# Queue orders rewritten: the opening of a conditioned attention and convolution block on one core

## The reference

```python
# 1. conditional 1x1 mixing: a small MLP of cond gives 8 weights per batch
att = softmax(gelu(gelu(cond @ W0 + b0) @ W1 + b1) @ W2 + b2)
agg = einsum('bk,koi->boi', att, weight);  y = einsum('boi,bih->boh', agg, x) + att @ bias_k
# 2. attention within each row: 32 heads of width 32, one shared key and value
q, k, v = y @ Wq + bq, y @ Wk + bk, y @ Wv + bv
o = einsum('bsde,bse->bsd', softmax(q_d * k_e / sqrt(32)), v)
x = x + broadcast(o)                 # q is summed over its 32 heads
# 3. grouped convolution (9 taps, 4 groups) + context of cond + bias, then a 4-bit linear layer
u = conv(x, weight2) + cond @ c_weight + bias
x = x + u @ (scale * (unpack(packed) - zero_point)).T + ffn_bias
```

## Time and profile before

| | before |
|---|---|
| median of three runs | 423.92 us |
| lowest, highest | 418.14, 425.28 us |
| span of the profiled execution, first to last instruction | 422.5 us |
| PE busy in it | 408.1 us, 97% |
| DVE, POOL, ACT busy | 356.2, 357.4, 222.6 us |

### The profile page before, as it was taken

One profiled execution on the slowest core, in us unless ns is written; L12 is line 12 of the kernel. 1 busy time (PEld: TensorE's weight loads), 2 busy tenths in 40 slices (PEclk: granted clock), 3 DMA queues, 4 the chain that ended last, 5 costly groups with the idle time before them and its releaser, 6 DMA issues.

```text
span 422.5 us, 6627 instructions
## 1 busy us (share of the span) xinstructions
PE 408.1 (97%) x2135; PEld 346.0 (82%) x2135; DVE 356.2 (84%) x594; ACT 222.6 (53%) x472; POOL 357.4 (85%) x358
## 2 busy tenths in 40 slices
PE   5979999999899999999999999999999999999997
PEld 4869988888788888888888888888888888888886
DVE  2679899999989999998979999989889899983422
ACT  4522896644637653774273565645463556572700
POOL 6034998999899999999998999999998889999920
PEclk9998999999999999999999999999999999999999
DMA  8984869067956036663069472919083452716112
GB/s 315 406 341 141 325 219 322 3 205 278 311 197 242 5 111 223 166 212 95 36 201 369 135 302 78 346 23 310 5 305 122 110 221 57 273 44 234 52 51 101
DMA packets 24954, 79.13 MB, mean 187 GB/s; under 512 B 6088, under 2 KB 6728, under 8 KB 22984
## 3 DMA queue, kind: packets, MB, share of 16 engines
q1 hardware_dynamic: 24760, 78.32, 52.9%
q10 hardware_dynamic: 144, 0.13, 0.1%
HBM read 61.14 MB, written 17.30 MB: 186 GB/s over the span
## 4 chain that ended last, share of the span: by engine, by line
PE 72%; DMA 2%; POOL 1%; DVE 1%; issue 1%; SPq 0%; DVEq 0%; POOLq 0%
PE p_f L1520 48%; PE p_conv L1514 18%; PE p_sm L1479 5%; DMA o_c<-o_dram 1%; PE p_sm L1499 1%; DMA o_dram<-o_sb 1%; PE p_conv L1520 0%; POOL c_lo L555 0%; DVE prob L1061 0%; POOL xc L545 0%; POOL xn L564 0%; DVE rden L1110 0%; POOL xc L548 0%; POOL xc L546 0%; DVE xn L1140 0%
## 5 line engine op out<-in xcount | busy, mean ns | idle before, releaser
L1520 PE MATMUL p_f<-w_ffn,u_hi 128*128 128x512 f32 (+1 forms) x512 | 194.7, 391 | 0.0
L1520 PE MATMUL p_f<-w_ffn,u_lo 128*128 128x512 f32 (+1 forms) x512 | 194.5, 389 | 0.0
L781 ACT ACTIVATE u_sb<-p_conv,u_bias,cols_sb 128x128 f32<-128x128 f32 x256 | 94.9, 461 | 37.9 <-PE p_conv L1514 37.5
L1520 PEld LDWEIGHTS p_f<-w_ffn,u_hi 128*128 128x128 f32 x512 | 96.2, 188 | 20.7 <-DVE u_lo L1130 0.3
L1520 PEld LDWEIGHTS p_f<-w_ffn,u_lo 128*128 128x128 f32 x512 | 96.1, 188 | 20.1
L555 POOL TENSOR_TENSOR c_lo<-xc,c_hi 128x516 fp32r<-128x516 f32 (+1 forms) x68 | 83.9, 1244 | 5.2 <-POOL xc L548 1.9
L771 ACT ACTIVATE c_hi<-xc 128x516 fp32r<-128x516 f32 (+1 forms) x68 | 41.4, 611 | 69.7 <-POOL xc L548 69.7
L564 POOL TENSOR_TENSOR xn<-xn,bias_n 128x1024 f32<-128x1024 f32 x32 | 76.4, 2404 | 0.2
L545 POOL TENSOR_TENSOR xc<-xc,o_c 128x384 f32<-128x384 f32 (+1 forms) x68 | 58.0, 853 | 7.9 <-DMA o_c<-o_dram 5.2
L1140 DVE TENSOR_TENSOR xn<-p_f,xn 128x512 f32<-128x512 f32 x64 | 43.2, 675 | 21.9 <-PE p_f L1520 21.5
L571 POOL TENSOR_TENSOR xn<-xn,o_sb 128x1024 f32<-128x1024 f32 x32 | 60.9, 1920 | 0.3
(11 more groups left out here) (127 smaller groups left out, 480.2 us busy)
## 6 DMA issues: line engine op xcount, KB each, us to landing
xn<-xn_in_in SPq DMA_DIRECT2D x16, 1024.0 KB, 6.9
out<-xn SPq DMA_DIRECT2D x31, 512.0 KB, 5.6
xc<-xc_in_in SPq DMA_DIRECT2D x15, 1032.0 KB, 8.7
xt<-xt_in_in SPq DMA_DIRECT2D x11, 1024.0 KB, 7.6
o_c<-o_dram SPq DMA_DIRECT2D x15, 256.0 KB
xn<-xt_in_in SPq DMA_DIRECT2D x3, 1024.0 KB, 15.2
xn<-wq_in SPq DMA_DIRECT2D x5, 512.0 KB, 8.4
xt<-xt_in_in SPq DMA_DIRECT2D x4, 512.0 KB, 9.7
```

The costliest lines, as they stand in the source:

```text
L781: ins = eng.activation(u_sb[:, g % 2, i * P:(i + 1) * P], p_conv[g % 2][:, i * P:(i + 1) * P], ACT.Identity, bias=u_bias[:, g, bat:bat + 1 ...
L1520: return mm(ffn_ps(k, part), u[:, (k // TU) % 2, r, t * P:(t + 1) * P], w_ffn[:, r, at:end], **flags)
```

## The change

The same sums are computed, with the same tiles. What differs:

- **PE.** `keep_busy` writes to bank `p_conv[1]`. Six dummy products behind `turn_att` become fifteen single ones: one behind `mlp(0)`, seven behind `mlp(2)`, two behind `turn_att`, and two, two and one between the z products of tile 0. `context` goes to bank `p_ut[0]`, waits for the copies of the mixing matrices out of it, and moves behind the first half of unit 3. `z_first` and `z_second` no longer wait for `u_bias`. `mix_first` moves ahead of `z_second`, `read_flag` behind the first half of unit 4.
- **DVE.** `logits` stands ahead of `sum_heads(0)`, the flag behind the last head sum. The maxima of tile 0 stay in PSUM (`top()`) instead of going to the SBUF tile `top_own`. `low_nibbles` stands ahead of `score(1, 0)`.
- **ACT.** `copy_vk` between the second `gelu` and `exp_att`; all four `mix_rows` ahead of `z_copy_first`; `bias_of_u` behind `exp(0, 1)`; `exp(1, 0)` and the first conversion ahead of `z_copy(3)`.
- **POOL.** `ones` is set first. All four `add_o(0, g)` run ahead of `c_low(0, 0)`, and three `add_o(1, g)` ahead of `c_low(0, 2)`.
- **SP.** The convolution weights are loaded two places sooner, the second half of unit 0's convolution input ahead of `spread_first(0)`, `bias` later.
- **All queues** are written out to the end, without the loops, and differ from before in many places: the number of each kind of call is the same, save the dummies; x of units 11 to 13 and 15 is projected somewhat sooner among the linear tiles, and POOL's last three additions of o stand together at its end.

The diff, cut to what the text speaks of:

```diff
             load_tile(1, 0)
+            load_conv_weights()
             load_tile(1, 1)
             load_x(2)
-            load_conv_weights()
             load_x(3)
             load_x(4)
             load_packed()
             save_o(0, 0)
             load_c_first(0)
+            load_c_first(1)
             spread_first(0)
             load_x(5)
-            load_bias()
             load_x(6)
             save_o(0, 1)
-            load_c_first(1)
+            load_bias()
             spread_first(1)
+            load_n(0)
             load_x(7)
-            load_n(0)
             save_o(1, 0)
             load_c(1)
             save_o(1, 1)
             spread_o(1)
             load_x(8)
+            load_x(9)
+            load_x(10)
             load_c(2)
             load_n(1)
+            store(0)
...
+            eng.memset(ones[:, :], 1.0).then_inc(s_ones, 1)
             eng.memset(ident[:, :], 0.0).then_inc(s_ident, 1)
             eng.wait_ge(s_ident, 1)
             eng.affine_select(out=ident[:, :], in_=ident[:, :], compare_op=ALU.not_equal, fill=1.0,
                               base=0, pattern=[[-1, P]], channel_multiplier=1).then_inc(s_ident, 1)
-            eng.memset(ones[:, :], 1.0).then_inc(s_ones, 1)
...
             add_o(0, 2)
+            add_o(0, 3)
             c_low(0, 0)
             c_low(0, 1)
             subtract(1, 1)
-            add_o(0, 3)
-            c_low(0, 2)
-            c_low(0, 3)
             add_o(1, 0)
             add_o(1, 1)
             add_o(1, 2)
+            c_low(0, 2)
+            c_low(0, 3)
+            add_o(1, 3)
             c_low(1, 0)
             c_low(1, 1)
-            add_o(1, 3)
             c_low(1, 2)
             x_bias(0)
+            x_o(0)
             c_low(1, 3)
-            x_o(0)
             add_o(2, 0)
...
+            x_bias(30)
+            c_low(16, 2)
+            c_low(16, 3)
+            x_bias(31)
+            x_o(29)
+            x_o(30)
+            x_o(31)
...
-                    eng.activation(u_bias[:, g, :], p_conv[1][:, B * g:B * g + B], ACT.Identity, bias=cbs[:, g:g + 1], scale=sc).then_inc(s_ub, 1)
+                    eng.activation(u_bias[:, g, :], p_ut[0][:, B * g:B * g + B], ACT.Identity, bias=cbs[:, g:g + 1], scale=sc).then_inc(s_ub, 1)
 
             gelu(0)
             gelu(1)
+            copy_vk()
             exp_att()
             slices()
-            bias_of_u()
             keep_bias()
-            copy_vk()
             keep_mix_bias()
             mix_rows(0)
             mix_rows(1)
             mix_rows(2)
+            mix_rows(3)
             z_copy_first()
-            mix_rows(3)
             z_copy(0)
             exp(0, 0)
             exp_first()
             z_copy(1)
             z_copy(2)
             exp(0, 1)
+            bias_of_u()
+            exp(1, 0)
+            convert_weights(0, 0)
             z_copy(3)
-            convert_weights(0, 0)
             z_copy(4)
             c_high(0, 0)
-            exp(1, 0)
             c_high(0, 1)
             convert_weights(0, 1)
+            u_copy(0, 0)
+            u_copy(0, 1)
+            exp(1, 1)
             c_high(0, 2)
-            u_copy(0, 0)
-            z_copy(5)
-            u_copy(0, 1)
             c_high(0, 3)
-            exp(1, 1)
-            u_high(0, 0)
             convert_weights(1, 0)
             c_high(1, 0)
+            c_high(1, 1)
+            c_high(1, 2)
+            z_copy(5)
+            z_copy(6)
+            u_high(0, 0)
+            u_high(0, 1)
...
-                eng.tensor_tensor(top_of(0)[:, 0, :], top()[:, 0, :], top2[:, 0, :], ALU.max).then_inc(s_top_first, 1)
+                eng.tensor_tensor(top()[:, 0, :], top()[:, 0, :], top2[:, 0, :], ALU.max).then_inc(s_top_first, 1)
...
-                eng.tensor_tensor(prob[:, t, d, :], prob[:, t, d, :], down(top_of(a)[:, t, d]), ALU.subtract).then_inc(s_sub, 1)
+                eng.tensor_tensor(prob[:, t, d, :], prob[:, t, d, :], down((top() if a == t == 0 else top_of(a))[:, t, d]), ALU.subtract).then_inc(s_sub, 1)
...
-                eng.tensor_tensor(prob[:, 0, FIRST, :], prob[:, 0, FIRST, :], down(top_of(0)[:, 0, FIRST]), ALU.subtract).then_inc(s_sub_first, 1)
+                eng.tensor_tensor(prob[:, 0, FIRST, :], prob[:, 0, FIRST, :], down(top()[:, 0, FIRST]), ALU.subtract).then_inc(s_sub_first, 1)
...
+            logits()
             sum_heads(0)
-            logits()
             normal()
             sum_heads(1)
-            mark_inexact()
             sum_heads(2)
             sum_heads(3)
             sum_heads(4)
@@ -1174,6 +1400,7 @@
             sum_heads(6)
             sum_heads(7)
             sum_heads(8)
+            mark_inexact()
             bias_of_qkv(0)
             softmax_top_first()
             score_first()
@@ -1190,100 +1417,99 @@
             divide(0, 0)
             score(0, 1)
             softmax_top(1)
+            low_nibbles()
             score(1, 0)
-            low_nibbles()
             sum_exp(0, 1)
             times_v(0, 1)
             sum_v(0, 1)
             divide(0, 1)
+            sum_exp(1, 0)
             score(1, 1)
-            sum_exp(1, 0)
+            times_v(1, 0)
+            high_nibbles()
+            sum_v(1, 0)
+            divide(1, 0)
             softmax_top(2)
-            high_nibbles()
-            times_v(1, 0)
-            sum_v(1, 0)
+            sum_exp(1, 1)
             turn_u(0, 0)
-            divide(1, 0)
-            sum_exp(1, 1)
+            times_v(1, 1)
             turn_u(0, 1)
-            times_v(1, 1)
+            sum_v(1, 1)
             u_low(0, 0)
-            sum_v(1, 1)
-            turn_u(0, 2)
             u_low(0, 1)
             divide(1, 1)
+            turn_u(0, 2)
...
-                    mm(p_conv[0][:, 0:P], ones[:, :], ones[:, :], start=True, stop=True)
+                    mm(p_conv[1][:, 2 * P:3 * P], ones[:, :], ones[:, :], start=True, stop=True)
...
-                    eng.wait_ge(s_ub, G)
...
-                eng.wait_ge(s_ub, G)
...
                 eng.wait_ge(s_ctx, 1)
+                eng.wait_ge(s_mixt, 2)
                 for g in range(G):
-                    last = mm(p_conv[1][:, B * g:B * g + B], ctx_sb[:, g, :, :].rearrange("p r c -> p (r c)"), cond_sb, start=True, stop=True)
+                    last = mm(p_ut[0][:, B * g:B * g + B], ctx_sb[:, g, :, :].rearrange("p r c -> p (r c)"), cond_sb, start=True, stop=True)
                 last.then_inc(s_cb, 1)
...
             mlp(0)
+            keep_busy(1)
             mlp(1)
             mlp(2)
-            context()
+            keep_busy(1)
+            keep_busy(1)
+            keep_busy(1)
+            keep_busy(1)
+            keep_busy(1)
+            keep_busy(1)
+            keep_busy(1)
             turn_att()
-            keep_busy(6)
+            keep_busy(1)
+            keep_busy(1)
             mixing(0)
             mixing(1)
             mixing(2)
             mixing_bias()
             mixing(3)
-            read_flag()
             z_first(0)
             z_first(1)
             z_first(2)
             z_first(3)
+            keep_busy(1)
+            keep_busy(1)
             z_first(4)
             z_first(5)
+            keep_busy(1)
+            keep_busy(1)
             z_first(6)
+            keep_busy(1)
             z_first(7)
             col_sum(7)
+            mix_first()
             z_second()
-            mix_first()
             mix(0)
             project(1, 0)
             project(1, 1)
@@ -1665,97 +2050,98 @@
             project(2, 0)
             project(2, 1)
             project(3, 0)
+            context()
             project(3, 1)
             mix(2)
             project(4, 0)
+            read_flag()
             project(4, 1)
             project(5, 0)
             conv(0, 0)
+            conv(0, 1)
             project(5, 1)
-            conv(0, 1)
             project(6, 0)
+            project(6, 1)
             conv(0, 2)
-            project(6, 1)
             conv(0, 3)
             project(7, 0)
             conv(1, 0)
+            conv(1, 1)
             mix(3)
-            conv(1, 1)
-            conv(1, 2)
             linear(0, 0)
             linear(0, 1)
             linear(0, 2)
-            conv(1, 3)
...
```

More of the change, by code:

```diff
@@ L1796, in _ @@
             linear(9, 6)
+            mix(8)
+            conv(7, 0)
             linear(9, 7)
-            conv(7, 0)
-            conv(7, 1)
             linear(10, 0)
@@ new lines, in _ @@
+            linear(15, 1)
+            mix(11)
+            linear(15, 2)
+            linear(15, 3)
+            linear(15, 4)
+            linear(15, 5)
+            linear(15, 6)
+            linear(15, 7)
+            linear(16, 0)
+            linear(16, 1)
+            linear(16, 2)
+            linear(16, 3)
+            linear(16, 4)
+            linear(16, 5)
+            conv(10, 0)
+            linear(16, 6)
+            linear(16, 7)
+            linear(17, 0)
+            conv(10, 1)
@@ new lines, in _ @@
```

(19 more changed lines are left out.)

1118 lines of the change are left out of this document (803 added, 315 removed).

## The result

| | median, us | runs |
|---|---|---|
| kernel before, beside it | 421.03 | 4 (416.49 to 425.28) |
| changed kernel | 424.06 | 4 (422.35 to 424.25) |

The ratio is 1.0144, 95% interval 1.0106 to 1.0182: slower by 1.4%, less than the 2% named above, but with the whole interval above 1. The forecast was 418.0, with a range from 412.5 to 424. The profiled execution took 424.25 with a span of 422.5, which is also the span that the prediction was worked out from.

The account below looks back on a forecast made before the run. PE, busy 408.1 of 422.5 us, was taken as the bound, POOL and DVE close behind. Span: 422.5 - 4.9 (opening) - 0.9 (47 to 120) = 416.7; against the median 423.92 - 5.8 = 418.1, stated 418.0, range 412.5 to 424.

Parts of the forecast that it names:

- the 2% named above: Whole kernel: what a measurement can tell, here 8.5 us.
- The opening, step by step: Start to conv(1, 0): hand-worked new times, first mix 20.3 against 24.20, conv(1, 0) 53.7 against 58.65; PE 4.9 us ahead.
- that choice between two bounds: Opening, z products of tile 0: clock rises before the last sums, giving 19.2 to 20, not about 23 at low clock.
- the 0.9 of that term: From 47 to 120 us: half of 1.7 us of c_low waits taken away; bounds 0 and 1.7.
- From 120 on ... I take 0: Behind 120 us: PE has no idle time to lose; DVE's and POOL's idle time covers the new order, 0 us.
- the mark itself: Behind 120 us: PE idle time there was listed among the signs that the forecast is wrong.
- the offset to the median: Whole kernel: runs' median 1.4 us above the profiled span, lowest run 4.4 below; forecast taken against the median 423.92.
- The PSUM maxima: DVE's first subtraction in the opening: one operand in PSUM avoids POOL's split, 0.68 instead of 2.81, giving back 2.13 us.
- the second rival: Opening gains, middle takes it back: clock rises no earlier, POOL bounds 47 to 120; 421 to 423 us, chance 0.20.
- The slower rival: POOL's queue: c_low(0,2) late behind adds and a DMA trip, PE waits at conv(0,2); e.g. 433 us, chance 0.08.
- three engines are within 3% of one another: Whole kernel: argument against the rival that all of the gain arrives, 414.8 us by the median, chance 0.30.

Follow-up runs that it names:

- the second profile: Changed kernel run once more without an edit: median 423.44 us, the profiled execution 422.62 with a span of 420.8.
- The new opening by itself: Changed kernel's opening on every queue to about the first linear slots of tile 0, then the order of before: 418.14 us, ratio 0.9986 to before.
- The kernel with two fillers: Changed kernel with two of its fifteen dummy products, both behind turn_att: 425.62 us, ratio 1.0147 to before.
- for the sums: Changed kernel with add_o(u, 2) behind c_low(u, 0) and add_o(u, 3) behind c_low(u, 1) in every unit: 436.57 us, ratio 1.0416 to before.
- The order up to tile 13: Changed kernel's lists to linear(13, 7), about 215 us, then what remains in the order of before: 420.03 us, ratio 1.0030 to before.
- both edits: Kernel before plus five dummy products, context product behind project(3, 0) in another bank, bias_of_u behind exp(0, 1): 417.36, again 416.95 us.
- loosened waits alone: Kernel before with the context product behind project(3, 0) in another bank and bias_of_u behind exp(0, 1), no added dummies: 419.03 us, ratio 1.0010.
- u_high moved: Changed kernel with u_high(11, 2), (11, 3), (12, 3) and (13, 3) ahead of the next unit's c_high on ScalarE: 427.84 us, ratio 1.0244 to before.
- GpSimd's old list: Changed kernel with only GpSimd's list behind linear(13, 7) in the order of before: 435.09 us, ratio 1.0354 to before.
- SyncE's old list: Changed kernel with only SyncE's DMA queue behind linear(13, 7) in the order of before: 445.42 us, ratio 1.0613 to before.

## Why the prediction was wrong

**The opening, step by step: right.** The sums ended at 18.53 (predicted 18.6), the first mix came at 19.47 (20.3), the first subtraction took 0.68 (0.68), mix 1 came at 26.51 with 0.42 of idle time (26.9, 0.4), the first half of unit 5 at 39.77 with 0.51 (40.3, 1.3), conv(0, 0) at 42.69 with 0.92 (42.8, 0.7), conv(0, 2) with 0.30 (0.5 to 0.8), conv(1, 0) at 53.20 (53.7). The clock rose at 12.5, ahead of the last sums; that choice between two bounds was right. From conv(1, 0) to 120 us the waits for c_lo shrank from 1.7 to 0.7 (one, at 66 us), so the 0.9 of that term arrived as well.

**First failed step: "From 120 on ... I take 0".** Its reasoning was that the idle time of DVE and POOL, 18.4 and 12.3 us, would cover any new order. Idle time summed over 260 us covers nothing: what counts is whether each single hand-over is in time, and the new order has four that are not, behind 120 us. The term measures 4.17 us of stands and 1.7 of the clock's fall behind the last. With the lead of 5.45, the 0.9 and these two the sum is 422.5 - 5.45 - 0.9 + 4.17 + 1.7 = 422.0, against 422.5 measured; 0.5 is left over. The stands come back in the second profile (3.94 us), the fall doesn't, and nine of ten executions had none, so it is the stands that carry the loss. The prediction said that the new order could only add idle time here, and gave no upper bound for it. The diff reordered five lists behind 120 us, and each crossing in them could have been followed as those of the opening were. The prediction named the mark itself: idle time of PE after 120.

**Second failed step: the offset to the median.** The opening's gain was measured from one execution of before, whose clock rose at 22. The prediction saw that the rise was late, and that the lowest run lay 4.4 under this span, but took the lateness for a property of the code. It was a property of the execution: with the rise at 13, the same code has its first mix at 20.64 and conv(1, 0) at 52.45. Of the 4.73 by which the first mix came earlier, 3.56 comes with the early rise in the old order too, and 1.17 is the order; of the 5.45 at conv(1, 0), 6.2 comes with the early rise (and the stand, the fall and the held subtraction that it avoids), and the order gives -0.75. The prediction also set times beside spans. In 108 of 109 executions of before whose span is on record, the time is 1.8 to 1.9 above the span, so the span of 422.5 belongs to a time of about 424.3, and the lowest run was about 6 below it, not 4.4: a stronger sign that this execution was not the usual one. The new opening by itself took 418.14, with no execution of ten above 420.76, and is worth nothing more.

**The PSUM maxima: right in mechanism, nothing in size.** They were credited with 2.13. With an early clock the subtraction with its SBUF operand takes 0.68 too, as POOL's split isn't there yet. The pair 2.81 and 0.68 of the earlier trace rows, which the prediction compares, has both inputs in SBUF in both rows, so it shows what the split does and not what PSUM does. Nor does the changed kernel show that, as its subtraction starts at 22.71, ahead of the split at 22.84. The kernel with two fillers does: its clock rises late, and both subtractions start inside the split and take 0.68. DVE and POOL there:

```profile
23.98 0.68 DVE L1317 TENSOR_TENSOR prob<-prob,p_sm 128x512 f32<-128x512 f32 x1
24.58 0.68 DVE L1293 TENSOR_TENSOR prob<-prob,p_sm 128x512 f32<-128x512 f32 x1
```

```profile
22.78 2.36 POOL L620 TENSOR_TENSOR cw_lo<-cw,cw_hi 128x1024 fp32r<-128x1024 f32 x1
```

The Trainium skill (SBUF, Who interferes with whom) says that a DVE instruction with at most one SBUF input doesn't contend with GpSimd, unless it runs in a mode that uses both ports, and that tensor_tensor has no such mode; these rows agree.

**The rivals.** The middle did take the gain back, as the second rival said, but not in its way: the clock rose early, POOL's queue in 47 to 120 was in time, and the loss came behind 120. The slower rival put one stand at conv(0, 2); it was 0.30. None had the loss where it was. The remark that three engines are within 3% of one another holds in neither stretch, and least behind 120 us, where PE has 260.0 us busy, POOL 247.7 and DVE 241.6 (5 and 7% less); in 47 to 120 they are within 3.5%.

**What stays open.** Which exchange in the new body costs each of the 3.4 us isn't settled: each list was put back, alone or in a group, and each time other stands came up. So no one of these lists can be named as the cause; single exchanges were tried only for u_high and for the sums. The order up to tile 13 may cost 1 to 2 us, by stands for c_lo at 43, 51, 67 and 134 us, but about 1 us of the first came with that execution's late trip of o, and the interval (1.0030 with 0.9984 to 1.0075) doesn't prove a loss. Why six of ten executions of the changed kernel take 1.5 us more than the other four wasn't seen. What makes the clock's rise late in one execution of before and not in another wasn't seen, only that with both edits no execution above 419.25 came up in 24.

## What to carry to other kernels

Before a gain is worked out from one profiled execution, look where that execution lies among the runs: if it is 4 us or more above the lowest, find what it has that the others lack, since a change that removes just this brings less than the profile promises. Where an order is changed on all engines, follow every crossing (who stands behind a waiting instruction) to the end; the average idle time of a queue is no cover. The lists of these engines were arranged together and couldn't be put back one by one; what helped was a small change in a working set, the fillers and the one moved product.

## What the runs showed of the hardware

- TensorE went over from 1.2 to 2.4 GHz at 22 and at 13 us in two executions of the same code, with nearly the same work before it (19 instructions of PE between 8 and 12 us in the one, 18 in the other). The column of the windows says 1.00 in both even before that; only the count of instructions shows it (12 and 21 from 18 to 20 us).
- 1.2 us after the end of a stand of 1.91 us the clock fell to 0.50 for 3.41 us. A fall of the same length came 0.4 us after the end of a stand of 2.24 (new opening, old body) and 0.9 us after one of 1.52 (loosened waits alone), and none came after one of 2.46 (u_high moved, clock 1.000 over the span). In the stands of 4.85 us (GpSimd's old list) and of 8.67 and 9.82 us (SyncE's old list) the clock fell while PE still stood, for 6.8 and twice for 10.2 us in all.
- In three executions with the same lists so far, o's first trip back from DRAM was asked for at 30.76, 30.94 and 31.35 us, and POOL waited 0.36, 1.21 and 2.27 us for it; PE's first product of the convolution then stood 0.92, 2.00 and 2.24 us.
- A subtraction on DVE of 128x512 took 2.81 us when it started 0.08 us into a GpSimd operation of 2.35 us and both its inputs were in SBUF, and 0.68 us when it started 1.20 us into such an operation with one input in PSUM.
